# A four-layer graph network on one core: the first layer's x loaded turned, its low part made on GpSimd, the c rows made from V, other load order and places

## The reference

```
L0: q,k,v = x W^T + b;  softmax over j of q.k/sqrt(32), masked where adj + I is 0;  8 heads
    x = layernorm(x + (attn v) Wo^T + bo) * gamma + beta
L1: q,k,v = x W + b;  scores + a_i + c_j + log(adj + 1e-9), a = x w_g[:256], c = x w_g[256:]
    x = x + softmax(scores) v
L2: f = x W_fc + b;  logits = f w_q + (f w_k)^T, masked by adj, leaky relu;  x = x + softmax(logits) f
L3: as L0, with log(max(adj, 1e-8)) added in place of the mask
```

## Time and profile before

| | us |
|---|---|
| median of 3 runs (1909.35 to 1915.19) | 1913.1 |
| profiled execution | 1908.63 |
| its span, first to last instruction | 1906.8 |
| PE busy | 1745.8 |
| DVE busy | 1550.6 |
| POOL busy | 1230.1 |
| ACT busy | 1216.3 |

### The profile page before, as it was taken

How to read it: one execution, slowest core, us unless ns; L and a number is a source line. 1 busy time by engine, 2 the same in 40 slices (tenths; PEclk the granted TensorE clock), 3 DMA queues, 4 the chain that set the end, 5 groups by cost and what they waited for, 6 DMA issues and landing times.

```text
span 1906.8 us, 54647 instructions
## 1 busy us (share of the span) xinstructions
PE 1745.8 (92%) x23564; PEld 1334.6 (70%) x23564; DVE 1550.6 (81%) x2976; ACT 1216.3 (64%) x1894; POOL 1230.1 (65%) x743
## 2 busy tenths in 40 slices
PE   3899998899999999889999989888999999988996
PEld 2667776677777777577777767667777677766774
DVE  2889887777799988777889988777788998877775
ACT  1567665467777775456877767546777776654675
POOL 2534588368874377728895348754888445883688
PEclk9999999999999999999999999999999999999999
DMA  5110000100221001000111000010021100001001
GB/s 138 40 40 18 13 18 29 41 19 29 63 68 35 13 18 35 17 29 24 51 57 62 24 19 13 30 45 7 19 74 57 51 19 13 18 29 40 13 18 46
DMA packets 67731, 66.44 MB, mean 35 GB/s; under 512 B 6050, under 2 KB 67492, under 8 KB 67492
## 3 DMA queue, kind: packets, MB, share of 16 engines
q1 hardware_dynamic: 67492, 62.95, 11.1%
HBM read 54.54 MB, written 8.39 MB: 33 GB/s over the span
## 4 chain that ended last, share of the span: by engine, by line
PE 74%; DVE 19%; ACT 2%; issue 2%; SPq 1%; POOL 1%; DMA 0%; DVEq 0%; POOLq 0%; ACTq 0%
PE gx L589 22%; PE sc L694 16%; PE od L727 16%; PE gx L740 5%; PE gx L614 3%; PE sc L688 3%; DVE ring L969 3%; PE sc L700 3%; PE gx L776 3%; DVE negm L941 2%; DVE negm L944 2%; DVE qk L923 2%; PE gx L707 2%; DVE lg L1013 1%; DVE negm L957 1%
## 5 line engine op out<-in xcount | busy, mean ns | idle before, releaser
L574 POOL TENSOR_TENSOR ring<-ring,adj_c 128x1024 f32<-128x1024 f32 x256 | 610.4, 2409 | 170.0 <-ACT ring L837 113.0
L694 PE MATMUL sc<-qk 32*128 32x256 f32 x9216 | 417.4, 297 | 11.2 <-ACT m_rows L827 4.4
L694 PEld LDWEIGHTS sc<-qk 32*128 32x128 f32 x9216 | 326.0, 187 | 110.1 <-issue 64.3
L824 ACT ACTIVATE aside<-sc 128x1024 f32<-128x1024 f32 x192 | 196.6, 1024 | 236.1 <-PE sc L694 156.3
L941 DVE TENSOR_REDUCE negm<-sc 128x4 f32<-128x1024 f32 x192 | 234.1, 1219 | 86.2 <-PE sc L694 51.8
L839 ACT ACTIVATE ring<-sc 128x1024 f32<-128x1024 f32 x256 | 248.4, 1023 | 29.8 <-PE sc L700 29.3
L727 PE MATMUL od<-ring,vf 128*32 128x256 f32 x3072 | 243.4, 388 | 3.2 <-POOL ring L574 3.2
L553 POOL TENSOR_TENSOR xs<-xs,bo 128x512 f32<-128x512 f32 x96 | 128.0, 1333 | 182.0 <-DVE xt_lo L915 169.4
L727 PE MATMUL od<-ring,ones_r 128*32 128x256 f32 x3072 | 236.1, 379 | 0.0
L944 DVE TENSOR_REDUCE negm<-aside 128x4 f32<-128x1024 f32 x192 | 232.3, 1210 | 0.0
L579 POOL TENSOR_TENSOR xs<-xs,lr_g 128x512 f32<-128x512 f32 x64 | 86.9, 1357 | 169.8 <-ACT xs L846 169.8
(11 more groups left out here) (141 smaller groups left out, 4320.5 us busy)
## 6 DMA issues: line engine op xcount, KB each, us to landing
adj_c<-in_adj_t SPq DMA_DIRECT2D x96, 256.0 KB, 2.8
adj_r<-in_adj SPq DMA_DIRECT2D x64, 256.0 KB, 2.9
xs<-in_x SPq DMA_DIRECT2D x32, 256.0 KB, 3.1
out<-xs SPq DMA_DIRECT2D x32, 256.0 KB, 2.2
wo<-in_w_o SPq DMA_DIRECT2D x2, 256.0 KB
ring<-in_w_q SPq DMA_DIRECT2D x2, 256.0 KB, 6.5
ring<-in_w_k SPq DMA_DIRECT2D x2, 256.0 KB, 6.7
lr_g<-in_w_bg SPq DMA_DIRECT2D x2, 128.0 KB
```

Of the source, the lines that this page charges most:

```text
L574: pool.tensor_tensor(part, part, adj_c[i.mi % 3][:, t, :].unsqueeze(1).to_broadcast([P, G, N]), ALU.mult).then_inc(weighted, 1)
L694: mm = pe.matmul(sc[:, g, t * N:(t + 1) * N], buf[rows, a, c, t * P:(t + 1) * P], buf[rows, b, c, :], start=(n == 0 and not masked), stop= ...
L824: act.activation(aside[:], sc[:, 0:2, :], ACT.Copy).then_inc(set_aside, 1)
```

## The change

1. **x turned on load.** The host hands over `x_t` too. For layer 0 a new SP step LT loads it into `x_raw` (two buffers); PE's T is gone there, ACT copies the high part from `x_raw` and POOL subtracts. Layers 1 to 3 keep their T.
2. **c rows from V.** `cr_hi`, `cr_lo`, `row_sel` and six matmuls per item go. A new step O: DVE copies the c column of V (`vf`) into `c_pad` and subtracts for the low part (both in SBUF), PE turns it with two matmuls against the identity, ACT copies to `c_rows`.
3. **First loads.** ACT issues weights 0 to 2 and the two first biases. SP starts with `x_raw` of item 0, `adj_r` of item 0, the eight loads that the bias fold needs (`fold_plain`, with its own semaphore), `x_raw` of item 1; the other 15 small loads and weights 3 to 9 follow the x of item 1. POOL's scaling of two biases moves to PC of item 1.
4. **Places.** All tables have other numbers; GAT_START is 25 for 24, LAST_START 37.5 for 33.5.

```diff
-    "T": {PE: [-1.369], ACTE: [-0.812], DVE: [-0.531]},
+    "T": {ACTE: [-2.091], POOL: [-2.032]},
 ...
+    "O": {PE: [3.901], ACTE: [3.712], DVE: [2.701]},
 ...
+            sp.dma_start(x_raw[0][:], x_t_all[items_l0[0].batch]).then_inc(xt_loaded[0], 16)
+            sp.dma_start(adj_r[0][:], adj_all[rows_of[0].batch]).then_inc(adjr_loaded[0], 16)
+            for dst, src in fold_plain:
+                sp.dma_start(dst, src).then_inc(w_fold, 16)
+            sp.dma_start(x_raw[1][:], x_t_all[items_l0[1].batch]).then_inc(xt_loaded[1], 16)
             for s, i, c in order[SP]:
-                if s == "LX":
+                if s == "LT" and i.i0 >= 2:
+                    sp.wait_ge(*x_split(items_l0[i.i0 - 2]))
+                    sp.dma_start(x_raw[i.i0 % 2][:], x_t_all[i.batch]).then_inc(xt_loaded[i.i0 % 2], 16)
+                elif s == "LX":
 ...
-                    if i.k == 0:
-                        for dst, src in first_plain:
-                            sp.dma_start(dst, src).then_inc(w_first, 16)
-                        for n in range(3):
+                    if i.k == 1:
+                        for dst, src in plain:
+                            sp.dma_start(dst, src).then_inc(w_plain, 16)
+                        for n in range(3, len(WEIGHTS)):
                             load_weight(n)
 ...
+                elif s == "T":
+                    pool.wait_ge(xt_hi_set, i.k + 1)
+                    pool.tensor_tensor(xt_lo[i.k % 2][:], x_raw[i.i0 % 2][:], xt_hi[i.k % 2][:].bitcast(F32), ALU.subtract)\
+                        .then_inc(x0_lo_set, 1)
 ...
-                        project(gx_of("ca", i)[:, 0:N], [lambda h: cr_hi[:, h, :], lambda h: cr_lo[:, h, :]],
-                                [lambda h: xh[:, h, :], lambda h: xl[:, h, :]]).then_inc(gx_sem("ca", i), 1)
 ...
+                elif s == "O":
+                    pe.wait_ge(c_pad_set, i.i1 + 1)
+                    pe.wait_ge(*gx_emptied("ca", i))
+                    for n in range(T):
+                        mm = pe.matmul(gx_of("ca", i)[:, n * P:(n + 1) * P], c_pad[i.i1 % 2][:, n, :], ident_r[:], start=True, stop=True)
+                    mm.then_inc(gx_sem("ca", i), 1)
 ...
+            for n in range(3):
+                if n == 1:
+                    for dst, src in first_plain:
+                        act.dma_start(dst, src).then_inc(w_first, 16)
+                name = WEIGHTS[n]
+                act.dma_start(staged[name][:, :, 0:D], w[name].rearrange("(c p) e -> p c e", p=P)).then_inc(w_raw[n], 16)
             split(0)
 ...
+                    if i.l == 0:
+                        act.wait_ge(xt_loaded[i.i0 % 2], 16 * (i.i0 // 2 + 1))
+                        if i.k >= 2:
+                            j = items[i.k - 2]
+                            what = "fp1" if j.l == GAT else "vb" if j.l == 1 else "v"
+                            act.wait_ge(gx_sem(what, j), gx_count(what, j))
+                        act.activation(hi, x_raw[i.i0 % 2][:].rearrange("p c n -> p (c n)"), ACT.Copy).then_inc(xt_hi_set, 1)
 ...
+                elif s == "O":
+                    gate_c = vf[i.mi % NVF][:, :, D + 1:D + 2].to_broadcast([P, T, G])
+                    pad = c_pad[i.i1 % 2][:].rearrange("p t (g r) -> p t g r", g=G)
+                    dve.wait_ge(v_set, v_count(i))
+                    if i.i1 >= 2:
+                        dve.wait_ge(c_set, i.i1 - 1)
+                    dve.tensor_copy(pad[:, :, :, 0], gate_c).then_inc(c_hi_set, 1)
+                    dve.wait_ge(c_hi_set, i.i1 + 1)
+                    dve.tensor_tensor(pad[:, :, :, 1], gate_c, pad[:, :, :, 0].bitcast(F32), ALU.subtract).then_inc(c_pad_set, 1)
```

More of the change, by code:

```diff
@@ L53 @@
[L53 to L58, removed]
+    "T": {ACTE: [-2.091], POOL: [-2.032]},
+    "Q": {PE: [0.397], ACTE: [0.988], DVE: [0.727]},
+    "P": {PE: [1.276], ACTE: [1.28], DVE: [0.899]},
+    "V": {PE: [2.592], ACTE: [3.47], DVE: [-13.074]},
+    "S": {PE: [3.267, 5.367], ACTE: [3.67, 5.365], DVE: [4.269, 5.695]},
+    "U": {DVE: [6.38002]},
+    "M": {PE: [8.17502], ACTE: [8.97702]},
@@ L76 @@
+    "N": {DVE: [14.687, 16.524]},
+    "F": {PE: [18.869]},
+    "XB": {POOL: [10.862]},
+    "H": {DVE: [18.738]},
+    "LC": {SP: [-1.485]},
+    "PC": {POOL: [3.355]},
 }
 MHA_PLAN3 = {
[L78 to L82, removed]
-    "U": {DVE: [6.406]},
@@ new lines @@
+    "V": {PE: [5.833], ACTE: [6.208], DVE: [-10.713]},
+    "S": {PE: [3.41, 5.618], ACTE: [4.033, 6.093], DVE: [4.673, 5.575]},
+    "U": {DVE: [6.299]},
+    "M": {PE: [8.176], ACTE: [7.949]},
+    "E": {PE: [8.679, 9.85], ACTE: [8.514, 10.649], POOL: [8.634, 10.263], DVE: [10.46, 10.865]},
+    "A": {PE: [11.35, 13.423, 13.608, 14.344]},
+    "N": {DVE: [13.757, 14.478]},
+    "F": {PE: [19.188]},
+    "XB": {POOL: [3.681]},
+    "H": {DVE: [19.363]},
+    "LC": {SP: [0.366]},
+    "PC": {POOL: [2.245]},
@@ L106 @@
-    "LR": {SP: [-11.454]},
-    "PR": {POOL: [-3.015]},
+    "LT": {SP: [-10.005]},
+    "LX": {SP: [-3.325]},
+    "LR": {SP: [-1.358]},
+    "PR": {POOL: [-1.441]},
 }
@@ L214, in gnn_stack @@
             plan_gx(GX_STAGES[stage], i)
-            if stage == "P" and i.l == 1:
-                plan_gx("ca", i)
         elif stage == "F":
@@ L523, in _ @@
             pool.tensor_scalar(b_col["q0"][:], b_col["q0"][:], SCALE, None, ALU.mult).then_inc(cols_set, 1)
-            pool.wait_ge(w_plain, 16 * len(plain))
-            for name in ("q1", "q3"):
-                pool.tensor_scalar(b_col[name][:], b_col[name][:], SCALE, None, ALU.mult).then_inc(cols_set, 1)
             def diagonal(buf):
@@ L555, in _ @@
                 elif s == "PC":
+                    if i.k == 1:
+                        pool.wait_ge(w_plain, 16 * len(plain))
+                        for name in ("q1", "q3"):
+                            pool.tensor_scalar(b_col[name][:], b_col[name][:], SCALE, None, ALU.mult).then_inc(cols_set, 1)
                     buf = adj_c[i.mi % 3]
```

208 lines of the change are left out of this document (86 added, 122 removed).

## The result

The changed kernel takes 2074.8 us (median of four, 2072.92 to 2079.75), the kernel before 1911.9 beside it: ratio 1.0855, 95% interval 1.0829 to 1.0881. It is 163 us slower; the forecast was 1872. The profiled execution took 2075.0, its span 2072.8.

What follows compares the result with a forecast made beforehand. TensorE was taken to bound the kernel (92% busy, full in layers 0 and 3). 15.5 + 14.7 + 18.7 - 8 = 40.9 us off 1908.6 gave 1867.7, with 4.5 for the median 1872 us; range 1857 to 1889.

Steps and rivals of the forecast that it cites:

- The start: First loads: reordering starts the first projection near 8 us and gains 15.5 us, bounds 8 to 24.
- Layer 0's turn: Layer 0: 128 transposes leave PE, gaining 14.7 us at 0.49 us for each of 30 items.
- what leaves PE in layer 0 should therefore shorten the kernel by its whole length: Layer 0: PE, busy 138.95 of 140 us, sets the pace as long as DVE keeps up.
- The lead is some ten us: cover enough: Layer 0: POOL computes the low part 2.4 units of place before its projection, so PE need not wait.
- rival (a): Layer 0: DVE or a late POOL low part sets the pace; 14.7 us not gained, 1887, up to 1891; chance 0.18.
- layers 0, 2 and 3 keep nearly their order: All stages: reason given for pricing the moved places at 0, between 15 us lost and 15 won.
- Layer 1's c rows: Layer 1: two small matmuls replace six, gaining 18.7 us, less 8 us for delayed small DVE operations.
- rival (c): Layer 1: ring multiplies block O's DVE operations, 2.1 us each, delaying PE through U and M; 1926 at half blocked; chance 0.06.
- the blocked share of the earlier trace, 12%: Layer 1: small DVE operations lost 0.26 of 2.1 us each, used as evidence against wide blocking of O.
- M's wait for the bank of T: Layer 1: M waits 0.6 us for the next item's low part, at no cost since the projection waited anyway.
- the prediction's own upper bound: Layer 1: worst loss if each of 64 new DVE operations is blocked for a whole multiply, 134 us.
- Other places: All stages: the other moved places were priced at 0, between 15 us lost and 15 won, besides layer 1's stalls.

Runs made afterwards that it cites:

- loads_only: The kernel before with only the new order of the first loads: 1897.8 us, ratio 0.9900.
- loads_again: The kernel before with only the new order of the first loads, repeated for its profile: 1898.1 us, ratio 0.9906.
- turn_late: The changed kernel with the old tables, layer 0's T included, six-matmul c rows and layer 0's low part on DVE: 1914.9 us, ratio 0.9992.
- pc_late_out: The changed kernel with layer 0's POOL column mask (PC) at 6.1 for 4.388 and SP's stores (OUT) at 27 for 24: 2054.9 us.
- old_places_c: The changed kernel with the old tables for shared steps (layer 0's T and XB as changed) and six-matmul c rows; low part on GpSimd: 2013.3 us.
- y_act: The changed kernel with ScalarE's place of layer 0's Y back at 28.749 for 29.964: 2010.6 us, ratio 1.0488.
- no_o: The changed kernel without step O's two DVE operations (c rows zero): 2068.4 us, ratio 1.0801.
- lc_early: The changed kernel with layer 0's load of the turned adjacency back at its old SyncE place, -3.406 for 5.559: 2136.6 us, ratio 1.1157.
- old_places: The changed kernel's code, O included, with the old tables for shared steps; layer 0's T, LT and XB as changed: 2171.0 us, ratio 1.1312.
- y_pc_out: The changed kernel with y_act's and pc_late_out's place changes together: 1991.0 us, ratio 1.0374.

## Why the prediction was wrong

By its own steps:

*The start*, 15.5: right, 15.0 at the first M (45.7 for 60.7), and loads_only and loads_again show it as a whole, 18 to 20 us of the medians (12.0 of the profiled spans).

*Layer 0's turn*, 14.7: wrong, +32.7 instead. The first step, "what leaves PE in layer 0 should therefore shorten the kernel by its whole length", holds in the middle of the stage (17.0 us per item for 17.5 in the first group, 17.09 in turn_late), and PE's busy time in layer 0 fell by 12.6 us. Two other steps failed. "The lead is some ten us: cover enough" counted places of the tables as time. The low part's 1.27 us was sized right (median 1276 ns; forecast 1.33), but what stands in POOL's queue in front of it waits: for adj_c behind SP's store (pc_late_out: 20 us), and at the crossings between groups for more (old_places_c: 106 us with the old places). My rival (a) allowed 4 us for this. And the other places were priced at nothing because "layers 0, 2 and 3 keep nearly their order". At the ends of the stage, where items of the next layer or of another group run beside it, lie 24.8 us for 17.7 (second distance of group 1) and 20.1 for 17.4 (the last). PE's idle time in layer 0 grew by 45.2 us, of which the late low part is 19.6; the rest is in smaller waits, for ScalarE and DVE, that no run took apart.

The Trainium skill, page Trainium Kernel Development and Optimization, section Performance Expectations, says that matmul busy time is a bad metric for how close a kernel is to its roofline, because matmuls are pipelined, and that the weight loads' busy share is a good one. For the question asked here, which engine sets the pace, this case went the other way: with matmuls busy all of the window and weight loads 37.48 of 52.54 us, the pace followed the matmuls taken away.

*Layer 1's c rows*, 18.7 less 8: wrong, +114.2 instead. The named rival (c), small DVE operations blocked by the ring multiplies and passed on through U and M, is what happened, with the price right (2.23 us median, 2.29 at most, for a 2.1 loss) and the share wrong: 20 of 32 for O's subtraction. I took the blocked share of the earlier trace rows, 12%, for the new operations too. But the share isn't a rate at which random meetings occur: in every group the engines fall into nearly the same phase, and one and the same operation meets the multiplies in most items or in none (L963: median 2226 here; 175 with a maximum of 178 in y_act). The 12% were of the same kind: 8 of the 64 of the earlier trace rows were blocked, the other 56 free. Also, I looked for the block in O; no_o shows that O's own operations aren't needed for it. What set much of the phase was ACT's Y at 29.964 for 28.749, which I had not followed to POOL at all. A second step failed behind it: M's wait for the bank of T was put at 0.6 us and at no cost, because "the projection behind it waited for it anyway". With that low part behind a blocked U it came to 85.3 us in 24 waits, 3.6 us each.

Not all of the 114.2 us is waiting. PE's idle time in layer 1 grew by 76.8 us; the other 37.3 are PE's busy time, 475.4 for 438.1 us with 83 matmuls fewer on record. The mean granted clock of the stage (group 1, first to last M) was 0.84 for 0.97, and PE stood idle for a fifth of it. No run separates the two, so that the clock follows from the waits is likely and not shown; the prediction had no term for it.

The Trainium skill's port rule (SBUF — State Buffer, Who interferes with whom), cited in the prediction, held for O's subtraction in all 32 instances, the 20 blocked and the 12 free. For the tensor_scalar L975 it is less clean: 56 of its 64 begin inside a GpSimd instruction, and 7 of these took no longer than a free one (279 to 291 ns). By the rule each of these small operations could be blocked for a whole multiply, and the prediction's own upper bound was 134 us.

*Other places*, priced 0 with 15 either way: wrong by far. Y alone is 64 us, PC with OUT 20, lc_early shows one load's place to cost 62, and layer 3, whose own code is as before, lost 30.8. Only part of this is layer 3's places. The third distance is 4 to 6 us longer in all four groups; most of the rest is in the last two, and only in the three groups behind which another layer 0 begins (8.2 to 9.7 us in all, for 4.8 in the last group). Against that, the tables as a whole are worth 96 us to this code (old_places 2171.0, changed kernel 2074.8). A table fits the code and the phase that it goes with, and a part's price read with one table says little under another. With the old ones the ladder reads 1898 (loads), 1908 (x turned, DVE), 2013 (low part on GpSimd), 2171 (O).

*What stays open:* about half of the loss. y_pc_out, with both repairs, is still 75 us above the kernel before on its chip and 93 above the one with the loads alone. In layer 1 y_act is 55 us above before (550.3 for 495.5 over four groups), with 65.0 us of PE waits for T's bank. Layer 3 has its 30.8; at its last items the engine of the low part matters again, and in opposite ways: with the old tables layer 3 takes 119.4 us on GpSimd and 106.5 on DVE, with the new ones 115 and 124. And the two ends of layer 0. No run repaired these.

## What to carry to other kernels

Before moving an operation to an engine with an in-order queue, list what stands ahead of it in that queue and what each of those waits for: the lead is the time after the last of these waits, not the distance in the schedule. Small VectorE operations on SBUF in a chain that gates TensorE were cheap here or cost nearly a whole GpSimd instruction each, most of them together, by phase; ask what holds GpSimd's multiplies in place before adding to the chain or moving anything ahead of them. And look at a stage item by item: here the full engine did set the pace in the middle, and taking work off it paid there, while the ends of the stage, where two layers share the engines, lost more than the middle gained.

## What the runs showed of the hardware

- A 128x8 DVE subtraction took 173 to 178 ns in all 32 items of one kernel, and 2226 in the median of the other, for one place on ScalarE. The 20 slow ones began inside a GpSimd instruction and ended 26 to 36 ns after it.
- The same 128x512 subtraction on DVE took 681 ns in the median with an input in PSUM and 685 with both in SBUF (turn_late), where the longest took 2074 beside GpSimd's work; on GpSimd 1276.
- The granted clock fell to 0.86 in layer 1 (0.97 before), where PE stood idle for 31 of 156 us; its busy time rose to 125.02 us from 115.75 with 1712 matmuls recorded for 1726.
